# A scan kernel in rounds of six segments: the output projection and its addition one segment earlier, and tanh rows and two copies at other places on ScalarE

## The chip, the cores and the metric

The kernel runs on one core of one Trainium2 chip. The metric is device time in microseconds, the median of several executions. TensorE is called PE in the profile, VectorE DVE, ScalarE ACT, GpSimd POOL and SyncE SP.

## The reference

The input x is 8 sequences of 512 steps with 128 channels. The first layer is a selective state space block, the second a mixture of 16 experts. Both are added to x. What matters here is the first:

```python
x = layernorm(x)
xn = x * rsqrt(mean(x * x) + 1e-6) * norm_w
x_branch, gate = split(xn @ W_in.T)              # 256 and 256 channels
xc = silu(causal_conv(x_branch) + conv_b)
dt = soft_clamp(softplus(xc @ W_dt.T + b_dt), 0.001, 0.1, 0.5)
Bp, Cp = xc @ W_B.T, xc @ W_C.T                  # 16 states
dA = exp(soft_clamp(dt[..., None] * A, -8, 8, 0.5))   # soft_clamp is a tanh
def step(h, ...):                                # 512 steps, one after the other
    h = h * dA_t + dt_t * B_t * x_t              # h: 8 x 256 channels x 16 states
    nrm = sqrt(sum(h * h))                       # of each sequence
    h = where(t % 10 == 0, h * min(20 / nrm, 1), h)
    y = einsum('bdn,bn->bd', h, C_t) + D * x_t
x_out = y * silu(gate) @ W_out.T
return x + scale * x_out
```

Then x + x_out is normalised, routed by `Wg` to one expert each, and goes through `w1`, relu and `w2`.

## The kernel before

Every tenth step h is scaled by a factor of its own norm, so time is cut into 52 **segments** of 10 steps (the last has 2). Channels lie on the 128 partitions in two halves; with 16 states and 8 sequences there are 256 rows of state, each of 10 columns and one for the start value. Six segments make a **round** (`w`, 0 to 8; `s` is the segment's place in it, 0 to 5), and each round prepares the input of the next one (`v1`) and the one after that (`v2`), and finishes the output of the one before (`o = w - 1`).

One segment S runs like this. POOL forms B times u for segment S+1 in two products (`products`, L837), and multiplies the last states of segment S-1 by C (`c_last`, L851). ScalarE makes the decays in four pieces, `decay`, each an exp (L977) of what a row tanh (`row_tanh`, L1086) left in `z`. VectorE runs four scans (L1359), the first two of which find their decays ready, then gates y of S-1 (L1344), multiplies states by C (L1410), and reduces the norm (L1327). Before that ScalarE squares the last column in two pieces (L987), the second behind scan 3, and TensorE sums the squares over partitions (`norm_sum`, L1723). POOL takes the power -1/2 (`root`, L866), TensorE spreads the factor (`norm_spread`, L1729), and VectorE writes the new start values (`restart`, L1333), with which the next segment's scans begin. TensorE also sums the states of S-1 to y (`sum_y`, L1751 and L1763) ahead of the norm sum.

Every engine has one queue in the order in which the code is written, and waits on semaphores. There is no planner: the `if s == ...` branches in each engine's loop decide between which steps of the recurrence the work of the other rounds stands. That work is, for the parts that the change touches:

- `project_out(o)` (L1681): eight products of 128 columns of the gated y with `W_out`, on TensorE, into PSUM bank PA. It waits for the last gated y of round o and for the first dt tanh of `v1`, which reads that bank.
- `add_out(o)` (L1422): residual plus scaled projection, on VectorE, between the last C multiplications. Then `out_stats(o)`: mean and variance (L1257, L1262) between scan 0 and scan 1, and `out_pool(o)` on POOL between the two products: an add, a multiply, a power (L873) and a multiply (L875). `make_h2(o)` (L1059) on ScalarE uses them in s4.
- `ln_pool(v2, part)`: the same kind of small steps for the input's two norms; part 3 is L800 and L802.
- `evac_bc(v1)`: two copies (L1031, L1035) of B and C from PSUM, on ScalarE, between the fourth exp and the clamp of dt (L1046).
- Row tanhs: 32 rows a round. Half of them (`WHOLE`) are done once for all 60 steps, the others (`HALVES`) in two halves of 30.

TensorE's clock is kept up by products whose result nobody reads (`keep_clock`, L1746; `idle_products`, L1578) in s3, in segment 2 and in the last rounds.

Of the kernel before, what the change touches and what calls it, by code (L numbers as in the profile page):

```python
# [35 lines left out]
def mamba_moe(nc, x, norm_w, W_in, conv_w, conv_b, W_dt, b_dt, W_B, W_C, A_log, D_param, W_out,  # L36
# [8 lines left out]
    NWIN = (NSEG + SPW - 1) // SPW  # L45
# [27 lines left out]
    with ExitStack() as ctx:  # L73
# [217 lines left out]
        o = 0  # L291
        xs, o = take(z, o, E, CT, 2 * DM)
# [478 lines left out]
        def _(pool):  # L771
# [137 lines left out]
            for S in range(NSEG):  # L909
                w, s = place_of(S)  # L910
                v1, v2, o = w + 1, w + 2, w - 1
                if S > 0:
                    c_last(S - 1)
                if s == 5 and v1 < NWIN:
                    make_u(v1, 1)
                if v2 < NWIN:
                    if s == (0 if w > 0 else 1):
                        ln_pool(v2, 0)
                        ln_pool(v2, 1)
                    if s == (1 if w > 0 else 2):  # L920
                        ln_pool(v2, 2)
                    if s == 2:
                        ln_pool(v2, 3)
                if s == 4 and v1 < NWIN:
                    make_u(v1, 0)
                if S + 1 < NSEG:
                    products(S + 1, [0])
                    if s == 3 and v1 < NWIN:
                        split_c(v1)
                    if s == 3 and 0 <= o < NWIN - 2:  # L930
                        out_pool(o)
                    products(S + 1, [1])
                    root(S + 1)
# [6 lines left out]
        def _(act):  # L940
# [27 lines left out]
            def decay(G):  # L968

                S, g = G // NG, G % NG  # L970
                w, s = place_of(S)
                r0, r1 = GRAN[g]
                if s % HALF == 0:
                    act.wait_ge(tanh_done, max(tanh_at[w, k, s // HALF] for k in range(r0 // B, (r1 - 1) // B + 1)))
                at_least(act, gscan, G - 1)
                n = LAST_STEPS - 1 if S == LS else SEG
                act.activation(region(G)[:, 0:(r1 - r0) * SLOT].rearrange("p (r c) -> p r c", c=SLOT)[:, :, 1:1 + n],  # L977
                               zall[:, r0:r1, SEG * s:SEG * s + n], ACT.Exp, scale=16.0).then_inc(exp_done, 1)
# [117 lines left out]
            def first_half(v, k0, k1):  # L1096
                for k in HALVES[k0:k1]:
                    row_tanh(v, k, 0, HALF * SEG)

            def second_half(v, k0, k1):  # L1100
                for k in (list(range(NST)) if v == 0 else HALVES)[k0:k1]:
                    row_tanh(v, k, HALF * SEG, WIN)
# [5 lines left out]
            def opening_rows(k0, k1, t1):  # L1108
                for k in range(k0, k1):
                    row_tanh(0, k, 0, t1)  # L1110
# [28 lines left out]
            for S in range(NSEG):  # L1139
                w, s = place_of(S)  # L1140
                v1, v2, o = w + 1, w + 2, w - 1
                prep, ln, out_ = v1 < NWIN, v2 < NWIN, o >= 0

                if S == 0:
                    opening_rows(16, 27, WIN)
                decay(NG * S + 2)
                if S == 0:
                    opening_rows(27, 32, WIN)
                decay(NG * S + 3)

                if s == 0 and w > 0:
                    if prep:
                        silu_x(v1, 1)
                    second_half(w, 0, 2)
                elif s == 1 and prep:
                    half_tanh_dt(v1, 0)
                    half_tanh_dt(v1, 1)
                elif s == 2 and prep:
                    evac_bc(v1)
                    clamp_dt(v1)  # L1160
                elif s == 3:
                    if prep:
                        tanh_gate(v1, 0)
                        tanh_gate(v1, 1)
                    if w == NWIN - 1:
                        make_h2(o)
                    first_half(v1, 0, 1)
                elif s == 4 and out_:
                    make_h2(o)
                elif s == 5:  # L1170
                    whole(v1, 5, 7)

                if S + 1 < NSEG:
                    square_last(S, 0)

                if S == 0:
                    silu_x(1, 0)
                elif s == 0:
                    second_half(w, 2, 3)
                elif s == 1:  # L1180
                    second_half(w, 14, 15)
                elif s == 3:
                    first_half(v1, 1, 3)
                elif s == 4:
                    first_half(v1, 15, 16)
                elif s == 5:
                    whole(v1, 7, 8)

                if S + 1 < NSEG:
                    square_last(S, 1)  # L1190

                if S == 0:
                    silu_x(1, 1)
                if s == 5:
                    whole(v1, 8, 9)
                if s == 3 and ln:
                    evac_xT(v2)
                if s == (3 if w == NWIN - 1 else 4) and out_:
                    evac_h2T(o)

                if S + 1 < NSEG:
                    decay(NG * S + 4)
                    decay(NG * S + 5)

                if s == 0:
                    second_half(w, 0 if w == 0 else 3, 14)
                elif s == 1:
                    if prep:
                        log_dt(v1)
                    second_half(w, 15, 16)  # L1210
                elif s == 2:
                    if prep:
                        scale_dt(v1)
                    if ln:
                        norm_x(v2)
                        add_norm(v2)
                elif s == 3:
                    first_half(v1, 3, 15)
                elif s == 4:
                    if ln:  # L1220
                        silu_x(v2, 0)
                    whole(v1, 0, 5)
                elif s == 5:
                    whole(v1, 9, 16)

            evac_h2T(NWIN - 1)
            act_tail(act)
# [2 lines left out]
        def _(dve):  # L1230
# [270 lines left out]
            for S in range(NSEG):  # L1501
# [11 lines left out]
                    continue  # L1513

                scan(S, 0)
                if s == 3 and 0 <= o < NWIN - 2:
                    out_stats(o)
                scan(S, 1)
                if S == 0:
# [16 lines left out]
                n0 = 6  # L1536
                if S == 0:
                    make_xc(1, 0)
                elif s == 2 and out_ and w < NWIN - 1:
                    add_out(o)  # L1540
                elif s == 3 and prep:
                    make_gate(v1, 1)
                elif s == 4 and w + 3 < NWIN:
                    ln_in(w + 3)
                elif s == 5 and v2 < NWIN:
                    make_xc(v2, 0)
# [16 lines left out]
        def _(pe):  # L1563
# [235 lines left out]
            for S in range(NSEG):  # L1799
# [28 lines left out]
                if s == 0 and w > 0 and prep:  # L1828
                    project_dt(v1, 0, 0)
                    project_dt(v1, 1, 0)  # L1830
                if s == 2 and out_:
                    project_out(o, 0, TILES if w < NWIN - 1 else 2)
                if s == 3 and ln:
                    keep_clock(CBANK[1], S)
# [82 lines left out]
```

## Time and profile before

| | |
|---|---|
| median of 3 timed runs | 703.77 us (703.64 to 707.52) |
| profiled execution, its own time | 705.44 us |
| its span | 703.6 us |
| PE busy | 619.2 us (88%) |
| POOL busy | 580.6 us (83%) |
| DVE busy | 556.6 us (79%) |
| ACT busy | 518.4 us (74%) |
| mean granted clock of TensorE | 0.956 |

The span runs from the first instruction to the last. The recurrence runs from 35 us (the first L866) to about 573 us (the last); the experts follow. A share of busy time is a mean over stages, and TensorE's is made of pipelined products whose ends are modelled, so it doesn't say which engine sets the time. For that one has to see, segment by segment, who waits. The granted clock is given as a share of full speed: 1.00 is 2.4 GHz, 0.50 is 1.2 GHz.

### The profile page before, as it was taken

To read this page: it belongs to the slowest core of one execution; us is meant where nothing else is said; L and a number is where in the kernel's file an instruction comes from. 1 tells how busy PE (TensorE), PEld (TensorE's weight loads), DVE (VectorE), ACT (ScalarE), POOL (GpSimd) and SP (SyncE) were. 2 spreads that over 40 slices of the span, in tenths; PEclk is the share of its full clock that TensorE was granted. 3 is DMA by queue.
4 is the path that set the end of the run, shared out by engine and by line. 5 is a ranking of instruction groups with operands and counts; after the bars stand their busy time and mean duration, and the time that the engine had idled before them with its cause. 6 is when DMAs were issued, how large, how long until landed. Compare 5 with 4: busy or idle time off the path is not lost.

```text
span 703.6 us, 12853 instructions
## 1 busy us (share of the span) xinstructions
PE 619.2 (88%) x4108; PEld 479.8 (68%) x4108; DVE 556.6 (79%) x891; ACT 518.4 (74%) x1011; POOL 580.6 (83%) x411
## 2 busy tenths in 40 slices
PE   8589999999899999989999998989989894699774
PEld 6246666767677677767677677857767782589664
DVE  5567888999999999999999999989889985713221
ACT  3798978989989998998999899899978622112120
POOL 5088998999999999999999989999989971277775
PEclk9889989999999999999999999999999997599997
DMA  3241523226244423623441353316145304346541
GB/s 100 83 149 60 170 94 118 73 93 222 63 147 125 144 53 119 190 96 133 110 148 62 131 161 125 118 45 187 60 119 156 94 1 104 113 130 202 182 145 33
DMA packets 59978, 81.95 MB, mean 116 GB/s; under 512 B 14830, under 2 KB 40723, under 8 KB 59911
## 3 DMA queue, kind: packets, MB, share of 16 engines
q1 hardware_dynamic: 56400, 74.79, 34.1%
q0 software_dynamic: 2560, 6.08, 2.9%
q8 instruction: 33, 0.54, 0.3%
q10 hardware_dynamic: 950, 0.27, 0.2%
q14 instruction: 35, 0.28, 0.2%
HBM read 69.61 MB, written 11.72 MB: 116 GB/s over the span
## 4 chain that ended last, share of the span: by engine, by line
POOL 58%; issue 22%; PE 11%; DVE 4%; DMA 3%; POOLq 1%; ACTq 0%; SPq 0%; ACT 0%; DVEq 0%
POOL h L837 29%; POOL h L851 18%; POOL u L824 3%; PE ps L588 3%; PE ps L575 3%; POOL fac L866 1%; DMA z<-rows_d,gidx 1%; POOL lnp L798 1%; POOL rstd L873 1%; PE ps L1635 1%; PE ps L595 1%; POOL out_dram L398 1%; POOL cq L861 1%; PE ps L555 1%; POOL z L390 1%
## 5 line engine op out<-in xcount | busy, mean ns | idle before, releaser
L1359 DVE TENSOR_TENSOR_SCAN h<-ps,h 128x902 f32<-128x902 f32 x204 | 319.8, 1608 | 24.3 <-ACT ps L977 16.2
L837 POOL TENSOR_TENSOR h<-u,scr 128x1280 f32<-128x1280 f32 x104 | 283.6, 2744 | 2.4
L1751 PEld LDWEIGHTS ps<-h,ident 128*128 128x128 f32 x1632 | 225.2, 190 | 22.3 <-issue 17.8
L1751 PE MATMUL ps<-h,ident 128*128 128x160 f32 x1632 | 231.4, 300 | 1.1 <-issue 0.8
L1086 ACT ACTIVATE z<-dtb,asc 128x240 f32<-128x240 f32 (+3 forms) x432 | 201.6, 537 | 0.1
L977 ACT ACTIVATE ps<-z 128x820 f32<-128x820 f32 (+1 forms) x208 | 137.9, 687 | 32.4 <-DVE h L1359 28.7
L851 POOL TENSOR_TENSOR h<-h,scr 128x1280 f32<-128x1280 f32 (+1 forms) x52 | 138.0, 2655 | 0.7 <-DVE h L1375 0.7
L1410 DVE TENSOR_TENSOR h<-h,ps 128x640 f32<-128x640 f32 (+1 forms) x155 | 87.8, 577 | 0.5 <-issue 0.2
L1635 PE MATMUL ps<-xnT,wT 128*128 128x488 f32 x144 | 75.2, 636 | 0.0
L987 ACT ACTIVATE sqb<-h 128x208 f32<-128x208 f32 x102 | 44.9, 441 | 24.3 <-DVE h L1359 21.6
L390 POOL DMA_INDIRECT z<-rows_d,gidx x32 | 33.2, 1036 | 34.7 <-DVE gidx L496 25.3
L1723 PEld LDWEIGHTS ps<-sqb,sel 128*8 128x8 f32 x832 | 28.4, 90 | 47.0 <-ACT sqb L987 36.4
L1723 PE MATMUL ps<-sqb,sel 128*8 128x33 f32 x832 | 35.1, 195 | 28.6 <-ACT sqb L987 18.7
L866 POOL TENSOR_TENSOR fac<-s,neghalf_e 8x1 f32<-8x1 f32 x52 | 27.5, 530 | 34.2 <-DVE s L1327 33.4
L424 ACT COPY h<-ps 128x256 f32<-128x256 f32 x16 | 6.0, 373 | 60.0 <-PE ps L563 60.0
L1729 PEld LDWEIGHTS ps<-ident,fac 8*128 8x128 f32 x104 | 15.8, 189 | 39.7 <-POOL fac L866 36.8
L398 POOL DMA_INDIRECT out_dram<-z,sidx x32 | 32.0, 1000 | 12.6 <-issue 7.8
L1333 DVE SCALAR_TENSOR_TENSOR h<-ps,h 128x256 f32<-128x256 f32 x52 | 32.0, 615 | 11.6 <-PE ps L1729 11.1
L513 DVE TENSOR_SCALAR h<-ps 128x512 f32<-128x512 f32 x16 | 11.1, 692 | 34.4 <-PE ps L575 34.4
L1635 PEld LDWEIGHTS ps<-xnT,wT 128*128 128x128 f32 x144 | 27.1, 204 | 16.0 <-issue 14.1
L1654 PE MATMUL ps<-xc,wT 128*128 128x488 f32 x72 | 35.8, 621 | 0.4 <-DVE xc L1316 0.4
L824 POOL TENSOR_TENSOR u<-dtb,xc 128x488 f32<-128x488 f32 x18 | 22.2, 1234 | 16.0 <-DVE h L1489 16.0
(201 smaller groups left out, 812.8 us busy)
## 6 DMA issues: line engine op xcount, KB each, us to landing
scr<-b_d SPq DMA_DIRECT2D x52, 640.0 KB, 4.4
scr<-c_d SPq DMA_DIRECT2D x52, 320.0 KB, 4.2
z<-in_L_ffn_w_dram SPq DMA_DIRECT2D x32, 256.0 KB, 3.2
xx_d<-xx SPq DMA_DIRECT2D x8, 256.0 KB, 2.0
xxr<-xx_d SPq DMA_DIRECT2D x8, 256.0 KB, 2.6
rows_d<-h2b SPq DMA_DIRECT2D x16, 120.0 KB, 2.1
rows_d<-xxr SPq DMA_DIRECT2D x16, 120.0 KB, 2.2
out_dram<-xxr SPq DMA_DIRECT2D x16, 120.0 KB, 2.4
```

The lines of the kernel that those rows point to most:

```text
L390: pool.indirect_dma_start(xs[:, e, t, :], None, rows_d, bass.IndirectOffsetOnAxis(ap=gidx[:, i:i + 1], axis=0), bounds_check=TOK - 1, oob_ ...
L824: pool.tensor_tensor(u[:, v % 2, hf, :], dtb[:, v % 2, hf, :], xc[:, v % 3, hf, :], ALU.mult).then_inc(u_done, 1)
L837: pool.tensor_tensor(hr[:, hf * RH:(hf + 1) * RH, 1:SLOT].rearrange("p (n b) t -> p n b t", b=B), us.unsqueeze(1).to_broadcast([P, NST, B, ...
L851: pool.tensor_tensor(m, m, cc4[:, S % RING, :].rearrange("p (r t) -> p r t", t=SEG)[:, :, 0:n] .unsqueeze(1).to_broadcast([P, H, NP * B, n ...
L977: act.activation(region(G)[:, 0:(r1 - r0) * SLOT].rearrange("p (r c) -> p r c", c=SLOT)[:, :, 1:1 + n], zall[:, r0:r1, SEG * s:SEG * s + n ...
L987: act.activation(sq_r[:, r0 // B:r1 // B, :], rows(h, S % RING)[:, r0:r1, SEG].rearrange("p (r b) -> p r b", b=B), ACT.Square).then_inc(sq ...
L1086: act.activation(zrow[:, k, :, t0:t1], dtb[:, v % 2, hf, :].rearrange("p (b c) -> p b c", b=B)[:, :, 1 + t0:1 + t1], ACT.Tanh, scale=asc[: ...
L1359: dve.tensor_tensor_scan(hs, region(G)[:, 0:(r1 - r0) * SLOT], hs, 0.0, ALU.mult, ALU.add).then_inc(gscan, 1)
L1410: dve.tensor_tensor(m, m, ps[:, bk, c0:c0 + (n1 - n0) * BS].rearrange("p (r t) -> p r t", t=SEG)[:, :, 0:n] .unsqueeze(1).to_broadcast([P, ...
L1635: ins = pe.matmul(bankc((PA, PB)[hf]), wT[:, hf * TAPS + k, :], xnT[:, :, k:k + COLS], start=False, stop=(k == TAPS - 1))
L1723: ins = pe.matmul(ps[0:B, YB, NCOL:NCOL + SQC], sel[:, b, :], sq_b[:, b, :], start=(b == 0), stop=(b == B - 1))
L1751: pe.matmul(ps[:, YB, 0:H * BS], ident[:], hr[:, :, n * B:(n + 1) * B, 0:SEG], start=(n == 0), stop=False)
```

## The change

For rounds 1 to 7, `project_out` moves from s2 to s1, with `add_out` behind it, and the statistics (`out_stats`, `out_pool`) from s3 to s2 (rounds 1 to 7). The last two steps of `ln_pool` follow its third directly, in s1 for s2. On ScalarE the copies of B and C move ahead of the fourth exp of s2, two whole row tanhs come from s5 to ahead of the fourth exp of s0, and half rows move: out of s3's long run and of s0 before the squares, into s5 and s1. The same instructions are issued in all, on every engine.

```diff
@@ ln_pool(v2, 3) on POOL
                     if s == (1 if w > 0 else 2):
                         ln_pool(v2, 2)
-                    if s == 2:
                         ln_pool(v2, 3)
@@ POOL
-                    if s == 3 and 0 <= o < NWIN - 2:
+                    if s == 2 and 0 <= o < NWIN - 2:
                         out_pool(o)
@@ ScalarE, before the fourth exp
+                elif s == 0:
+                    whole(w, 14, 16)
+                elif s == 2 and prep:
+                    evac_bc(v1)
                 decay(NG * S + 3)
@@ ScalarE, behind it
                     if prep:
                         silu_x(v1, 1)
-                    second_half(w, 0, 2)
...
                 elif s == 2 and prep:
-                    evac_bc(v1)
                     clamp_dt(v1)
...
-                    first_half(v1, 0, 1)
@@ ScalarE, between the squares
-                    second_half(w, 2, 3)
+                    second_half(w, 0, 1)
                 elif s == 1:
-                    second_half(w, 14, 15)
+                    second_half(w, 14 if w == 0 else 12, 15 if w == 0 else 13)
                 elif s == 3:
-                    first_half(v1, 1, 3)
+                    first_half(v1, 0, 2)
                 elif s == 4:
-                    first_half(v1, 15, 16)
+                    first_half(v1, 12, 13)
@@ ScalarE, behind the next segment's first two exps
-                    second_half(w, 0 if w == 0 else 3, 14)
+                    second_half(w, 0 if w == 0 else 1, 14 if w == 0 else 12)
                 elif s == 1:
...
-                    second_half(w, 15, 16)
+                    second_half(w, 15 if w == 0 else 13, 16)
...
-                    first_half(v1, 3, 15)
+                    first_half(v1, 2, 12)
...
-                    whole(v1, 9, 16)
+                    whole(v1, 9, 14)
+                    first_half(v1, 13, 16)
@@ VectorE
-                if s == 3 and 0 <= o < NWIN - 2:
+                if s == 2 and 0 <= o < NWIN - 2:
                     out_stats(o)
...
-                elif s == 2 and out_ and w < NWIN - 1:
+                elif s == 1 and out_ and w < NWIN - 1:
                     add_out(o)
@@ TensorE
-                if s == 2 and out_:
+                if s == (1 if w < NWIN - 1 else 2) and out_:
                     project_out(o, 0, TILES if w < NWIN - 1 else 2)
```

TensorE, s1 and s2 of a middle round, before: in s1 the dt products (L1654) of s0, the sum of states, two spreads of C (L1738), the norm sum (L1723), and the products for B and C (L1664); then s2 with the projection (L1681) ahead of its norm sum and the gate product (L1649).

```order
L1654 MATMUL ps<-xc,wT 128x488 x2
L1751 MATMUL ps<-h,ident 128x160 x16
L1763 MATMUL ps<-xc,diag_d 128x80 x2
L1738 MATMUL ps<-c,ones_b 128x480
L1738 MATMUL ps<-c,ones_b 128x160
L1723 MATMUL ps<-sqb,sel 8x33 x8
...
L1751 MATMUL ps<-h,ident 128x160 x16
L1763 MATMUL ps<-xc,diag_d 128x80 x2
L1738 MATMUL ps<-c,ones_b 128x480
L1681 MATMUL ps<-wT,yg 128x128 x8
L1723 MATMUL ps<-sqb,sel 8x33 x8
```

The same place after, where every line number is one lower or higher (L1682 is the projection):

```order
L1655 MATMUL ps<-xc,wT 128x488 x2
L1752 MATMUL ps<-h,ident 128x160 x16
L1764 MATMUL ps<-xc,diag_d 128x80 x2
L1739 MATMUL ps<-c,ones_b 128x480
L1739 MATMUL ps<-c,ones_b 128x160
L1682 MATMUL ps<-wT,yg 128x128 x8
L1724 MATMUL ps<-sqb,sel 8x33 x8
...
L1752 MATMUL ps<-h,ident 128x160 x16
L1764 MATMUL ps<-xc,diag_d 128x80 x2
L1739 MATMUL ps<-c,ones_b 128x480
L1724 MATMUL ps<-sqb,sel 8x33 x8
```

The eight products went from between the sum of states and the norm sum of s2 to the same place in s1.

VectorE, from the end of s1 into s2, before: the reduction (L1327), C multiplications (L1410), restart (L1333) and scans (listed as L1359).

```order
L1327 TENSOR_REDUCE s<-ps 8x1
L1410 TENSOR_TENSOR h<-h,ps 128x2x16x10 x2
L1333 SCALAR_TENSOR_TENSOR h<-ps,h 128x256
L1359 SCALAR_TENSOR_TENSOR h<-ps,h 128x902
L1359 SCALAR_TENSOR_TENSOR h<-ps,h 128x506
L1359 SCALAR_TENSOR_TENSOR h<-ps,h 128x902
L1359 SCALAR_TENSOR_TENSOR h<-ps,h 128x506
```

And after, with the addition (L1423) and the statistics (L1258, L1263):

```order
L1328 TENSOR_REDUCE s<-ps 8x1
L1411 TENSOR_TENSOR h<-h,ps 128x2x16x10
L1423 SCALAR_TENSOR_TENSOR xxr<-ps,rs,xxr 128x512
L1411 TENSOR_TENSOR h<-h,ps 128x2x16x10
L1334 SCALAR_TENSOR_TENSOR h<-ps,h 128x256
L1360 SCALAR_TENSOR_TENSOR h<-ps,h 128x902
L1258 BN_STATS bst<-xxr 128x6 x4
L1261 MEMSET pad 128x1
L1263 BN_AGGR mv<-bst 128x2 x4
L1360 SCALAR_TENSOR_TENSOR h<-ps,h 128x506
L1360 SCALAR_TENSOR_TENSOR h<-ps,h 128x902
L1360 SCALAR_TENSOR_TENSOR h<-ps,h 128x506
```

The addition now stands ahead of the restart of s2, the statistics between its first two scans.

ScalarE, from the end of s5 into s0, before: whole row tanhs, the two exps (L977), the tanh of x (L1011), two half rows and the first squares (L987).

```order
L1086 ACTIVATE z<-dtb,asc 128x480 x7
L977 ACTIVATE ps<-z 128x82x10
L977 ACTIVATE ps<-z 128x46x10
L1011 ACTIVATE thx<-ps 128x488
L1086 ACTIVATE z<-dtb,asc 128x8x30 x2
L987 ACTIVATE sqb<-h 128x26x8
```

And after:

```order
L1085 ACTIVATE z<-dtb,asc 128x480 x5
L1085 ACTIVATE z<-dtb,asc 128x8x30 x3
L976 ACTIVATE ps<-z 128x82x10
L1085 ACTIVATE z<-dtb,asc 128x480 x2
L976 ACTIVATE ps<-z 128x46x10
L1010 ACTIVATE thx<-ps 128x488
L986 ACTIVATE sqb<-h 128x26x8
```

Two whole rows moved from before the two exps to between them, and the tanh of x stands behind them.

## Rows read from the trace of the kernel before

**Rows 1.** The page, part 4: the chain that ended last, by engine.

```profile
POOL 58%; issue 22%; PE 11%; DVE 4%; DMA 3%; POOLq 1%; ACTq 0%; SPq 0%; ACT 0%; DVEq 0%
```

**Rows 2.** Timeline, POOL, segments 25 to 30: start, length (us), operation, [idle before].

```profile
315.05 0.53 POOL L866 TENSOR_TENSOR fac<-s,neghalf_e 8x1 f32<-8x1 f32 x1
...
325.03 0.53 POOL L866 TENSOR_TENSOR fac<-s,neghalf_e 8x1 f32<-8x1 f32 x1 [0.80 <-DVE s L1327]
...
331.67 0.20 POOL L870 TENSOR_TENSOR ve<-mv,eps 128x4 f32<-128x4 f32 x1
...
333.22 2.74 POOL L837 TENSOR_TENSOR h<-u,scr 128x1280 f32<-128x1280 f32 x1
336.30 0.53 POOL L866 TENSOR_TENSOR fac<-s,neghalf_e 8x1 f32<-8x1 f32 x1 [0.34 <-DVE s L1327]
...
346.91 0.53 POOL L866 TENSOR_TENSOR fac<-s,neghalf_e 8x1 f32<-8x1 f32 x1 [0.83 <-DVE s L1327]
...
357.30 0.53 POOL L866 TENSOR_TENSOR fac<-s,neghalf_e 8x1 f32<-8x1 f32 x1 [0.48 <-DVE s L1327]
...
367.71 0.53 POOL L866 TENSOR_TENSOR fac<-s,neghalf_e 8x1 f32<-8x1 f32 x1
```

**Rows 3.** Timeline of PE (TensorE), segments 25 to 27, same columns.

```profile
314.09 0.66 PE L1723 MATMUL ps<-sqb,sel 128*8 128x33 f32 x16 [0.85 <-ACT sqb L987]
...
322.09 2.05 PE L1681 MATMUL ps<-wT,yg 128*128 128x128 f32 x16
324.07 0.66 PE L1723 MATMUL ps<-sqb,sel 128*8 128x33 f32 x16
...
335.35 0.66 PE L1723 MATMUL ps<-sqb,sel 128*8 128x33 f32 x16 [0.72 <-ACT sqb L987]
```

**Rows 4.** Timeline of DVE (VectorE), segments 25 to 30.

```profile
316.12 0.61 DVE L1333 SCALAR_TENSOR_TENSOR h<-ps,h 128x256 f32<-128x256 f32 x1 [0.36 <-PE ps L1729]
...
320.26 3.14 DVE L1359 TENSOR_TENSOR_SCAN h<-ps,h 128x902 f32<-128x902 f32 x2 [0.26 <-ACT ps L977]
...
326.33 0.60 DVE L1333 SCALAR_TENSOR_TENSOR h<-ps,h 128x256 f32<-128x256 f32 x1
...
329.01 0.85 DVE L1257 BATCH_NORM_STATS2 bst<-xxr 128x6 f32<-128x128 f32 x4
...
330.19 3.10 DVE L1359 TENSOR_TENSOR_SCAN h<-ps,h 128x506 f32<-128x506 f32 x2
...
342.44 3.14 DVE L1359 TENSOR_TENSOR_SCAN h<-ps,h 128x902 f32<-128x902 f32 x2 [0.88 <-ACT ps L977]
...
364.62 0.64 DVE L1316 SCALAR_TENSOR_TENSOR xc<-thx,ps 128x488 f32<-128x488 f32 x1
```

**Rows 5.** Timeline of ACT (ScalarE), segments 26 to 30.

```profile
322.81 0.92 ACT L987 ACTIVATE sqb<-h 128x208 f32<-128x208 f32 x2
...
336.93 4.74 ACT L1086 ACTIVATE z<-dtb,asc 128x240 f32<-128x240 f32 x12
...
363.06 0.55 ACT L1011 ACTIVATE thx<-ps 128x488 f32<-128x488 f32 x1
```

**Rows 6.** Windows (busy by engine, PEclk, DMA share, GB/s); then PE, POOL timeline.

```profile
91.80:95.20 3.40, 1.97 (x27) 1.46 (x25) 3.27 (x5) 2.11 (x5) 2.71 (x2) 1.00 0.00 0
95.20:102.00 6.80, 6.80 (x13) 3.38 (x13) 6.15 (x16) 4.97 (x9) 6.56 (x4) 0.50 0.43 149
...
399.00:402.40 3.40, 3.40 (x6) 1.33 (x5) 2.36 (x5) 3.40 (x9) 3.40 (x3) 0.50 0.08 18
...
94.40 0.66 PE L1723 MATMUL ps<-sqb,sel 128*8 128x33 f32 x16 [1.43 <-ACT sqb L987]
...
107.99 0.53 POOL L866 TENSOR_TENSOR fac<-s,neghalf_e 8x1 f32<-8x1 f32 x1 [2.73 <-DVE s L1327]
...
410.01 0.53 POOL L866 TENSOR_TENSOR fac<-s,neghalf_e 8x1 f32<-8x1 f32 x1 [1.50 <-DVE s L1327]
...
525.48 0.53 POOL L866 TENSOR_TENSOR fac<-s,neghalf_e 8x1 f32<-8x1 f32 x1 [1.89 <-DVE s L1327]
```

## The prediction

> **What bounds the kernel now.** I read three views. The chain that ended last is POOL for 58% of the span and "issue" for 22% [rows 1]: the two state products and the C product of each of 52 segments. But the chain alone misleads, so I went to the timeline of one round (segments 24 to 29, the fifth round). POOL's power L866 ends each segment, and its row tells who was late. I call its start the root, R, and the segments of a round s0 to s5. Where the row has no idle time, POOL was just in time or late itself; where it says "DVE s L1327", the recurrence was late: restart L1333, four scans L1359, squares on ACT, norm sum L1723 on PE, reduction L1327. From [rows 2], the root waits 0.80 us in s2, 0.34 in s3, 0.83 in s4, 0.48 in s5, and nothing in s1 and s0. So the work of POOL and the recurrence lie within a few tenths of each other everywhere, and anything put on the recurrence in any segment, or on POOL in s0 or s1, costs its full length. The segments last (root to root) 9.98 us in s2, 11.27 in s3, 10.61 in s4, 10.39 in s5, 10.41 in s0. s3 is the longest, and loses most to what the change takes out of it. Rounds 1 to 7 of 0 to 8 have the moved projection.
>
> **Projection to s1 (seven rounds).** Its eight products lie from 322.09 to the norm sum at 324.07, so they cost TensorE 1.98 us [rows 3]. In s2 they were nearly free: the squares end at 322.81 + 0.92 = 323.73 [rows 5], so the norm sum came only about 0.3 late. In s1 TensorE starts its sum of states later, since the dt products precede it, and had just 0.85 us idle before the norm sum at 314.09 [rows 3]. The projection needs only the first dt tanh and the last gated y of the round before, both there by then, and it is issued ahead of the norm sum on an engine that runs products in order. The norm sum, and behind it reduction, root and restart, come 1.98 - 0.85 = 1.13 us later; I take **+1.1** for s1. The two small POOL steps that come to s1 too (each like the 0.20 us add of 331.67 [rows 2], about 0.5 with issue) would by themselves have lengthened s1; behind 1.1 they are free.
>
> **Addition to s1, statistics to s2.** The addition stands between the last C multiplications and the restart. In s2 the restart began 326.33 - 325.03 = 1.30 after the root, in s1 316.12 - 315.05 = 1.07 [rows 2, 4]. So the addition brings s2 at most 0.23. What it gives back in s3 is nothing that I count, because TensorE's two gate products around the root set the restart there too. The statistics, between scan 0 and scan 1, take 330.19 - 329.01 = 1.18 us of VectorE [rows 4]. In s2 they come on top, but two waits go: 0.3 for the projection, and the wait of scan 2 for ScalarE's exp (0.26 idle in the row of 320.26, 0.37 with the pieces around it). Result on the recurrence: 1.18 + 0.23 - 0.3 - 0.37 = **+0.75**. POOL's statistics steps take 333.22 - 331.67 = 1.55 [rows 2]; against the 0.80 that POOL waits in s2, and the 0.5 that left for s1, they are +0.25 and covered. If the waits did not go, s2 would grow by 1.4; if the exp were late by the two more row tanhs, no more than that, as they run while VectorE does restart and scan 0, and TensorE's lateness in s1 has given ScalarE 1.1 us.
>
> **s3.** It loses 1.18 of statistics and, on POOL, 1.55. Without them POOL needs 11.27 - 0.34 - 1.55 = 9.4 and isn't the bound. The recurrence gets the 1.18, less a few hundredths in which ScalarE (its eight normalisations now stand directly before the exp of scan 2) may be late: **-1.15**.
>
> **ScalarE rows.** Twelve half rows ran before the exp of scan 2 in s4: 4.74 us, 0.395 each, and VectorE waited 0.88 for that exp [rows 4, 5]. Two leave: 2 x 0.395 = 0.79 < 0.88, and POOL would allow 0.83: **-0.79** in s4. They go to s5 (five whole and three half rows for seven whole: 3.0 + 1.2 = 4.2 us, the same) and s1. In s0 two whole rows (1.2 us) now stand before the second exp and the tanh of x. That tanh ran at 363.06 for 0.55 [rows 5]; it would end about 364.8, and the multiplication L1316 that waits for it began at 364.62 [rows 4], so it begins about 364.9: **+0.28**, with no slack to hide it in (the root of 367.71 did not wait, and POOL had only just finished). The copies of B and C move ahead of the second exp of s2, for which VectorE isn't ready until scan 1 ends. They and the clamp took 322.81 - 320.26 = 2.55 us at most [rows 4, 5]; in the new order the clamp ends before scan 2 does, so they cost nothing. If they did delay the squares, as much as 0.5 would show in s2.
>
> **Sum with the clock unchanged.** A round: 0.28 + 1.1 + 0.75 - 1.15 - 0.79 = +0.19. Rounds 1 to 6 give +1.1. Round 7 has no gain in s4 (POOL bounds it there): +1.0. Round 0 has only the row tanhs: -0.8. Together **+1.3 us**.
>
> **The clock.** In s2 TensorE now finishes its sums at about R + 7.0 (where the projection began, 322.09 - 315.05) and has nothing until the norm sum at R + 10.73 - 0.96 = R + 9.8: an idle stretch of **2.7 us**, in seven rounds. The windows view shows what shorter ones did. TensorE idled 1.43 us before the norm sum of 94.40, and the granted clock was 0.50 (1.2 GHz) from 95.20 to 102.00; after waits like the 0.72 of 335.35 it mostly stayed at 1.00, but one such round was at 0.50 from 399.00 to 402.40 [rows 3, 6]. What it cost is in the root's waits: 2.73 for 0.48 at 107.99, so 2.25 us; 1.50 for 0.83 at 410.01, so 0.7; and 1.89 for 0.34 at 525.48, so 1.55 [rows 2, 6]. A new fall of 3.4 us at half clock delays TensorE's work by up to 1.7 us. Of that s3 hides little, since without the statistics the sum of states, the clock keeper and the turn of x fill the time to the norm sum (its 0.72 shrinks to about 0.4): 1.3 each, between 0.7 (the row at 410.01) and 1.7. I take six falls in seven rounds: 6 x 1.3 = +7.8. The old three mostly go: s4 of round 0 is 0.79 shorter, with an idle stretch of 0.6 for 1.43 (-2.25); round 7 waited in s3 for a gate that now comes 1.15 earlier (-1.55); the third I count by half (-0.35). Net +3.7. The Trainium skill (TensorE: Matmul & The Clock Gate, Why this matters for your kernels) puts a fall down to a window in which TensorE is idle. Taken literally that would spare s2, where TensorE works on both sides of the gap; the row of 91.80 to 95.20, busy for 1.97 us of 3.40 ahead of a fall [rows 6], speaks against that reading. By the page the result would be the rival without falls.
>
> **Result.** +1.3 + 3.7 = +5. On the profiled execution, 705.44 us (its span 703.6 and 1.8 around it), that is 710.4. That execution lies 1.7 above the median of the three timed runs, 703.77; on the median it is 708.8, so **709 us**, with a range of its own of 705 to 713. A measurement of this kernel can tell about 1% (7 us) from no change.
>
> **Rivals.** (1) No falls, as the idle stretch is short of what the clock tolerates: 703.8 + 1.3 - 4.15 = **701**. For it: most 0.7 us waits cost nothing. Against: 1.43 did. (2) Slower: long falls. If a fall begins before the norm sum of s2 it still has idle time behind it, and then lasts 6.8 us like the one from 95.20; it halves the norm sum and both gate products around the root. Price up to 3.4 us less 0.4 a round; with four long and three short ones 4 x 3.0 + 3 x 1.3 = 15.9, so 703.8 + 1.3 + 15.9 - 4.15 = **717**. It decides from the point where the onset comes ahead of the norm sum. (3) Faster: the projection in s1 is hidden after all (TensorE gets through the sum of states earlier), 7 x 1.1 = 7.7 less than (1): **693**. For it only that the first tanh of dt is done early; against it TensorE's unbroken row of work before 0.85. (4) The change doesn't do what it says: a wait in s1 (for the residual's load or PSUM bank) keeps the addition late. The order shows the edits on all engines and the load is issued a segment earlier, so this stays small; with it every figure in s2 grows by a few tenths: 712.
>
> **Chances.** Forecast 0.47, (1) 0.22, (2) 0.18, (3) 0.08, (4) 0.05. Faster by over 1% (below 696.7) is (3) and a sliver of (1): 0.09. Slower by over 1% (above 710.8) is (2), a third of the forecast, and most of (4): 0.39. Within 1%: 0.52. The range for 8 in 10 leaves out (3) and the far end of (2): 699 to 718.
>
> **What would show it.** Root to root in a middle round: s1 about 10.8 (from 9.74), s2 10.7, s3 10.1 without a fall and 11.4 with one, s4 9.8, s0 10.7. The norm sum of s2 with some 2.7 us of idle TensorE before it, that of s1 directly behind the projection with none. A clock row with several slices below 9 between the start and the end of the recurrence. VectorE's 0.88 for the exp in s4 gone. I am wrong if the norm sum of s1 still waits for the squares, if s3 doesn't shrink by about 1.1, or if the clock holds through s2.

## The result, and the profile after

The changed kernel takes 713.5 us (median of 4 runs, 710.26 to 716.11); the kernel before, on the same chip, 704.16 (703.64 to 707.52, 4 runs). The ratio is 1.0129 [1.0076, 1.0182]: slower by 1.3%, about 9 us, just outside the 1% that the prediction took as what a measurement can tell. Forecast were 709, with 0.52 on "within 1%" and 0.39 on slower. One execution of a later kernel, e7_keep_silu, took 904.6 us at a mean granted clock of 0.644, and is left out of every range and ratio below.

| | before | after |
|---|---|---|
| profiled execution, its own time | 705.44 us | 710.26 us |
| its span | 703.6 | 708.5 |
| mean granted clock of TensorE | 0.956 | 0.951 |
| start of the last root | 572.82 | 577.80 |

The profiled execution of the changed kernel is the fastest of its four, while that of the kernel before lies 1.7 us above its median. So the two traces differ by 5 us and the medians by 9; the gap is taken up below.

The page after, its clock slices (part 2) and the chain that ended last (part 4), the latter beside [rows 1]:

```profile
PEclk9889999899999999999999899999999997599997
...
POOL 60%; issue 21%; PE 10%; DMA 4%; DVE 4%; POOLq 1%; ACTq 0%; SPq 0%; ACT 0%; DVEq 0%
```

The chain has nearly the same shares as before and says nothing of the change. The roots do. POOL's timeline, L866 from the end of s0 of round 2 to the end of s0 of round 3; start, length, operation, [idle before]:

```profile
179.42 0.53 POOL L866 TENSOR_TENSOR fac<-s,neghalf_e 8x1 f32<-8x1 f32 x1 [0.53 <-DVE s L1328]
...
190.22 0.53 POOL L866 TENSOR_TENSOR fac<-s,neghalf_e 8x1 f32<-8x1 f32 x1 [0.53 <-DVE s L1328]
...
200.93 0.53 POOL L866 TENSOR_TENSOR fac<-s,neghalf_e 8x1 f32<-8x1 f32 x1 [0.53 <-DVE s L1328]
...
211.00 0.53 POOL L866 TENSOR_TENSOR fac<-s,neghalf_e 8x1 f32<-8x1 f32 x1 [0.68 <-DVE s L1328]
...
220.84 0.53 POOL L866 TENSOR_TENSOR fac<-s,neghalf_e 8x1 f32<-8x1 f32 x1
...
231.23 0.53 POOL L866 TENSOR_TENSOR fac<-s,neghalf_e 8x1 f32<-8x1 f32 x1 [0.47 <-DVE s L1328]
...
242.01 0.53 POOL L866 TENSOR_TENSOR fac<-s,neghalf_e 8x1 f32<-8x1 f32 x1 [0.51 <-DVE s L1328]
```

Differences of these starts are the segments of an undisturbed round, against those that [rows 2] and the prediction give:

| segment | before | predicted | after | change, predicted | change, measured |
|---|---|---|---|---|---|
| s1 | 9.74 | 10.8 | 10.80 | +1.1 | +1.06 |
| s2 | 9.98 | 10.7 | 10.71 | +0.75 | +0.73 |
| s3 | 11.27 | 10.1 | 10.07 | -1.15 | -1.20 |
| s4 | 10.61 | 9.8 | 9.84 | -0.79 | -0.77 |
| s5 | 10.39 | 10.4 | 10.39 | 0 | 0 |
| s0 | 10.41 | 10.7 | 10.78 | +0.28 | +0.37 |

Without the clock a round grows by 0.19, as priced. The mechanisms are those that the prediction named, too. TensorE after, norm sums of s1, s2 and s3 of round 2, beside [rows 3]:

```profile
187.28 2.05 PE L1682 MATMUL ps<-wT,yg 128*128 128x128 f32 x16
...
189.26 0.66 PE L1724 MATMUL ps<-sqb,sel 128*8 128x33 f32 x16
...
199.97 0.66 PE L1724 MATMUL ps<-sqb,sel 128*8 128x33 f32 x16 [2.45 <-ACT sqb L986]
...
210.04 0.66 PE L1724 MATMUL ps<-sqb,sel 128*8 128x33 f32 x16 [0.33 <-ACT sqb L986]
```

In s1 the projection now stands directly ahead of the norm sum, and the 0.85 us of idle time is gone. In s2 the stretch without work is 2.45 us (2.7 was forecast). VectorE, from the reduction of s1 to the statistics of s2, beside [rows 4]:

```profile
189.96 0.18 DVE L1328 TENSOR_REDUCE s<-ps 8x1 f32<-8x33 f32 x1 [1.19 <-PE ps L1724]
...
190.47 0.73 DVE L1423 SCALAR_TENSOR_TENSOR xxr<-ps,rs,xxr 128x512 f32<-128x512 f32 x1
...
191.52 0.60 DVE L1334 SCALAR_TENSOR_TENSOR h<-ps,h 128x256 f32<-128x256 f32 x1
...
194.20 0.85 DVE L1258 BATCH_NORM_STATS2 bst<-xxr 128x6 f32<-128x128 f32 x4
```

The restart begins 191.52 - 190.22 = 1.30 after the root, as forecast, and the statistics stand between scan 0 and scan 1. In s0 the tanh of x is late, on VectorE:

```profile
238.89 0.66 DVE L1317 SCALAR_TENSOR_TENSOR xc<-thx,ps 128x488 f32<-128x488 f32 x1 [0.26 <-ACT thx L1010]
```

What is not as priced is the clock. A fall is a stretch in which the granted clock is 0.50; in the recurrence of all traces here, behind the first 43 us, it lasts 3.4 us (short) or 6.8 us (long). Round 1 has a long one. The windows view around it (us; busy time of PE, PEld, DVE, ACT, POOL; clock; DMA share; GB/s), and in the last two lines a short one of round 3:

```profile
130.60:134.00 3.40, 1.68 (x13) 1.31 (x11) 3.40 (x3) 2.64 (x4) 3.32 (x6) 1.00 0.31 83
134.00:140.80 6.80, 6.07 (x26) 3.42 (x27) 4.42 (x8) 5.53 (x12) 5.88 (x4) 0.50 0.36 118
140.80:144.20 3.40, 3.40 (x27) 3.40 (x25) 3.40 (x3) 2.46 (x4) 3.24 (x4) 0.99 0.79 269
260.40:263.70 3.30, 1.13 (x18) 0.92 (x19) 3.17 (x6) 2.55 (x6) 2.77 (x2) 1.00 0.74 244
263.80:267.10 3.30, 3.30 (x6) 1.33 (x5) 1.91 (x4) 3.30 (x8) 3.30 (x3) 0.50 0.16 53
```

And what the long one does to TensorE around the root, and then to the roots of s2, s3 and s4:

```profile
134.73 1.05 PE L1724 MATMUL ps<-sqb,sel 128*8 128x33 f32 x16 [2.45 <-ACT sqb L986]
...
135.95 2.00 PE L1650 MATMUL ps<-xnT,wT 128*128 128x488 f32 x2
137.88 0.59 PE L1730 MATMUL ps<-ident,fac 8*128 8x8 f32 x2
```

```profile
136.07 0.53 POOL L866 TENSOR_TENSOR fac<-s,neghalf_e 8x1 f32<-8x1 f32 x1 [0.92 <-DVE s L1328]
...
148.13 0.53 POOL L866 TENSOR_TENSOR fac<-s,neghalf_e 8x1 f32<-8x1 f32 x1 [2.68 <-DVE s L1328]
...
158.25 0.53 POOL L866 TENSOR_TENSOR fac<-s,neghalf_e 8x1 f32<-8x1 f32 x1 [0.34 <-DVE s L1328]
```

At 1.2 GHz the norm sum takes 1.05 us for 0.66, and the gate products hold the spread of the factor back to 137.88. s2 is 11.09 long for 10.71, s3 148.13 - 136.07 = 12.06 for 10.07, s4 10.12 for 9.84: 0.38 + 1.99 + 0.28 = **2.65 us for a long fall**. Rounds 1 and 5 have one. Rounds 3 and 4 have a short fall that begins behind the norm sum (s3 11.26 and 11.30, s4 10.12: 1.5 each), and round 7 a short one that costs 1.15. Rounds 2 and 6 have none, though TensorE idles the same 2.45 us in them. The falls of this trace add up to 9.4 us in five rounds, against 7.8 in six. One more thing differs between the two traces, and has nothing to do with the moved work: the kernel before has a short fall at 54 to 58 us, in segment 1 of the opening (root to root 13.05 us), and the changed kernel has none there (11.37).

### The profile page after: what moved, and what is told of

Its sections match the earlier page's. It is cut to its first block, busy times and chain, and to the rows that moved or that the text cites. A ratio compares the mean times of both kernels' runs of the same rounds, so it can differ in the third digit from the quotient of the medians.

```text
span 708.5 us, 12846 instructions
## 1 busy us (share of the span) xinstructions
PE 623.9 (88%) x4108; PEld 483.1 (68%) x4108; DVE 556.5 (79%) x891; ACT 521.1 (74%) x1011; POOL 580.6 (82%) x411
## 4 chain that ended last, share of the span: by engine, by line
POOL 60%; issue 21%; PE 10%; DMA 4%; DVE 4%; POOLq 1%; ACTq 0%; SPq 0%; ACT 0%; DVEq 0%
POOL h L837 31%; POOL h L851 18%; POOL u L824 3%; PE ps L588 3%; PE ps L575 3%; DMA z<-rows_d,gidx 2%; POOL fac L866 1%; POOL lnp L798 1%; POOL rstd L873 1%; PE ps L1636 1%; POOL z L390 1%; PE ps L555 1%; POOL cq L861 1%; POOL out_dram L398 1%; DMA b0b<-b_d 1%
## 5 line engine op out<-in xcount | busy, mean ns | idle before, releaser
L1752 PEld LDWEIGHTS ps<-h,ident 128*128 128x128 f32 x1632 | 227.5, 192 | 25.3 <-issue 19.6
L1636 PE MATMUL ps<-xnT,wT 128*128 128x488 f32 x144 | 72.2, 613 | 0.0
L866 POOL TENSOR_TENSOR fac<-s,neghalf_e 8x1 f32<-8x1 f32 x52 | 27.6, 531 | 39.6 <-DVE s L1328 39.4
```

The source lines that it names most:

```text
L1636: ins = pe.matmul(bankc((PA, PB)[hf]), wT[:, hf * TAPS + k, :], xnT[:, :, k:k + COLS], start=False, stop=(k == TAPS - 1))
L1752: pe.matmul(ps[:, YB, 0:H * BS], ident[:], hr[:, :, n * B:(n + 1) * B, 0:SEG], start=(n == 0), stop=False)
```

## Experiments

The first four kernels ran on one chip, the last four on another. On the first chip the kernel before took 713.58 us (25 runs, 709.61 to 718.2) instead of 704. Segments without a fall were as long there as elsewhere; from the last root to the end of the span it took 141 to 143 us instead of some 131, and the totals of one kernel lay up to 9 us apart. There the roots of the profile decide, and the totals tell little. Neither the kernel before nor the changed one has a profile from that chip, so roots are compared across chips; on the second chip (703.81 us, 12 runs, 701.87 to 705.45) both can be used.

| run | what it is | median, us (range) | ratio to before, same chip | last root |
|---|---|---|---|---|
| e1_keep | changed, s2 kept busy | 714.05 (710.22 to 717.89) | 0.9997 [0.9966, 1.0028] | 570.18 |
| e2_act_only | ScalarE's part alone | 713.26 (709.85 to 716.61) | 0.9983 [0.9955, 1.0012] | 567.76 |
| e3_out_only | the rest alone | 733.29 (731.84 to 736.41) | 1.0273 [1.0224, 1.0322] | 588.12 |
| e4_proj_end | projection at the end of s1 | 720.08 (715.86 to 724.9) | 1.0086 [1.0051, 1.0122] | 578.6 |
| e0_before | kernel before, one look | 705.89 | | 573.94 |
| e5_changed | the changed kernel | 711.96 (710.36 to 713.33) | 1.0117 [1.0085, 1.0149] | 579.01 |
| e6_two_rows | before, two half rows moved | 697.0 (695.84 to 700.7) | 0.9916 [0.9889, 0.9942] | 563.51 |
| e7_keep_silu | e1_keep, tanh of x first | 699.41 (697.52 to 702.1) | 0.9948 [0.9925, 0.9972] | 565.84 |

**e1_keep: is it the idle stretch of s2?** The changed kernel, with TensorE given products that nobody reads in that stretch.

```diff
+                if s == 2 and 0 < w < NWIN - 1:
+                    keep_clock(CBANK[1], S)
+                    keep_clock(CBANK[1], S)
```

> The changed kernel with two clock-keeping products of 512 columns (1.1 us each by the row of L1746) in s2 of rounds 1 to 7, between the spread of C and the norm sum, where TensorE is idle for 2.7 us. Theory (the loss beside the sum of the segments is TensorE's clock falling in that idle stretch): no falls in rounds 1 to 7, s1 10.8, s2 10.7, s3 10.1, s4 9.8 in every round, and about 701 us, 12 below the changed kernel and 3 below the one before. Rival (the clock is a symptom and the time is lost to the waits that were moved): about 713 as the changed kernel. If the products run into the norm sum, s2 grows by some tenths.

The idle stretch before the norm sum shrinks from 2.45 to 0.54 us. TensorE, s2 of round 2:

```profile
195.37 1.98 PE L1747 MATMUL ps<-wT,ones_w 128*128 128x512 f32 x4
197.89 0.66 PE L1724 MATMUL ps<-sqb,sel 128*8 128x33 f32 x16 [0.54 <-ACT sqb L986]
```

In rounds 1 to 6 no segment shows a fall any more: s1 10.80, s2 10.70, s3 10.07, s4 9.84 in each. Round 7 has none in s2 to s4 either, but one in s5 (11.10 us long; the clock is at 0.50 from about 534 to 537), which the expectation did not have. The clock slices show it:

```profile
PEclk9889999999999999999999999999999995799896
```

Its last root comes at 570.18, 7.6 us ahead of the changed kernel's 577.80, although its opening (segments 0 and 1) was 1.1 us longer. Adding that 1.1 and the 1.25 of the fall in s5 of round 7, less 0.55 for a first root that came earlier, gives 9.4, which is what the falls of the changed kernel's trace add up to. The filler delays nothing: s2 is as long as in an undisturbed round of the changed kernel. The total missed what was expected of it. Its level, 714 for 701, is the chip's, but the ratio missed too: 0.9997 where 3 us less than the kernel before were expected. The totals of that chip cannot tell the two apart well, and the same edit is timed again in e7_keep_silu.

**e2_act_only: ScalarE's part alone.** The kernel before, with ScalarE's hunks of the diff and nothing else.

```diff
@@ ScalarE: every hunk of the change; TensorE, VectorE and POOL as before
+                elif s == 0:
+                    whole(w, 14, 16)
+                elif s == 2 and prep:
+                    evac_bc(v1)
                 decay(NG * S + 3)
...
```

> The kernel before with only the changes on ScalarE (row tanhs, copies of B and C). Theory: s4 9.84 (-0.77), s0 10.77 (+0.36), the other segments as before, the fall of round 0 gone (-2.6 in s5): 704.2 - 0.8 - 2.6 - 6 x 0.41 + 0.4 = about 699 us. Rival (the rows in s1 and the copies ahead of the fourth exp cost the recurrence in s2): s2 10.3 to 10.8, and 701 to 704.

s4 is 9.84 and s0 10.77, as in the changed kernel, and no segment of rounds 1 to 7 shows a fall. But s2 is 10.46, not 9.98: there the rival was right. ScalarE, ahead of the exp of scan 2 in s2, then VectorE and POOL:

```profile
191.24 0.48 ACT L1086 ACTIVATE z<-dtb,asc 128x240 f32<-128x240 f32 x1
191.63 0.84 ACT L977 ACTIVATE ps<-z 128x820 f32<-128x820 f32 x1
```

```profile
192.49 3.14 DVE L1361 TENSOR_TENSOR_SCAN h<-ps,h 128x902 f32<-128x902 f32 x2 [1.03 <-ACT ps L977]
```

```profile
186.50 0.53 POOL L866 TENSOR_TENSOR fac<-s,neghalf_e 8x1 f32<-8x1 f32 x1
...
196.97 0.53 POOL L866 TENSOR_TENSOR fac<-s,neghalf_e 8x1 f32<-8x1 f32 x1 [1.28 <-DVE s L1329]
```

Before, scan 2 of s2 waited 0.26 for that exp and began 320.26 - 315.05 = 5.21 after the root [rows 2, 4]; here it waits 1.03 and begins 192.49 - 186.50 = 5.99 after it, since two more half rows stand ahead of the exp. In the changed kernel nobody notices: the root of s1 comes a microsecond later there, and the statistics keep VectorE busy in the meantime. The prediction had used that cover for its s2; the expectation for this run forgot that it goes when the ScalarE part stands alone. A term that is free only behind another term of the same change has to be priced again when the other is taken out.

**e3_out_only: the rest alone.** The changed kernel with ScalarE as before.

```diff
@@ TensorE, VectorE and POOL as in the change; ScalarE as before
-                if s == 2 and out_:
+                if s == (1 if w < NWIN - 1 else 2) and out_:
                     project_out(o, 0, TILES if w < NWIN - 1 else 2)
...
```

> The kernel before with only the changes on TensorE, VectorE and POOL (projection, addition, statistics, last norm steps), ScalarE as before. Theory: s1 10.8, s2 10.7 to 10.9, s3 10.1 without a fall and 11.3 to 12.1 with one, s4 stays 10.6, s0 10.4. 704.2 + 7 x 0.7 + falls of about 7 less 1.5 in round 7 = about 714 us. Rival (the row changes cause the falls or the late s1): about 704.

Undisturbed, s1 is 10.80, s2 10.78, s3 10.07, s4 10.61 and s0 10.41: the terms are additive where no cover is shared. The total is 19.7 us above the kernel before, where 10 were expected, and most of it is the clock. POOL, the ends of s2 to s5 of round 5:

```profile
395.45 0.53 POOL L866 TENSOR_TENSOR fac<-s,neghalf_e 8x1 f32<-8x1 f32 x1 [0.62 <-DVE s L1326]
...
408.34 0.53 POOL L866 TENSOR_TENSOR fac<-s,neghalf_e 8x1 f32<-8x1 f32 x1 [3.51 <-DVE s L1326]
...
419.23 0.53 POOL L866 TENSOR_TENSOR fac<-s,neghalf_e 8x1 f32<-8x1 f32 x1 [1.12 <-DVE s L1326]
...
432.88 0.53 POOL L866 TENSOR_TENSOR fac<-s,neghalf_e 8x1 f32<-8x1 f32 x1 [3.76 <-DVE s L1326]
```

s3 is 12.89 for 10.07, and s5 432.88 - 419.23 = 13.65 for 10.39: one segment loses 3.3 us, more than any of the changed kernel. Both are long falls, from 395 and from 419 us. That the second comes from the idle stretch of s4, which is long again with VectorE's wait for the exp, is my reading; no run varies that stretch alone. Read segment by segment, the falls of rounds 1 to 7 add up to 14.6 us in this kernel, against 9.4 in the changed one and 1.25 in e1_keep. The changed kernel differs from this one by ScalarE's part alone, so in these executions that part took some of the falls away.

**e4_proj_end: projection in the idle stretch of s1's end instead.** The changed kernel with the eight products behind the last product of s1, after the spread, and the addition in s2 between scan 0 and the statistics.

```diff
@@ TensorE
-                if s == (1 if w < NWIN - 1 else 2) and out_:
-                    project_out(o, 0, TILES if w < NWIN - 1 else 2)
+                if s == 2 and out_ and w == NWIN - 1:
+                    project_out(o, 0, 2)
...
+                if s == 1 and out_ and w < NWIN - 1:
+                    project_out(o, 0, TILES)
@@ VectorE: add_out(o) from s1 to s2, ahead of out_stats(o)
```

> The changed kernel with the projection behind the last product of s1 (after the norm spread) in place of ahead of the norm sum, and the addition in s2 between scan 0 and the statistics. Theory: s1 back to 9.8, s2 11.2 (the addition now lies between scans, +0.5), TensorE's sum of states in s2 starts 2 us later and fills the idle stretch down to 0.7 us, so no falls; s3 10.1, s4 9.8: 704.2 - 7 x 0.38 - 4.2 = about 697 us. Rival (TensorE is the bound in s2 once the projection precedes the sum of states): s2 over 11.5 and no gain over the kernel before.

This failed. TensorE and POOL, round 2:

```profile
192.03 1.95 PE L1681 MATMUL ps<-wT,yg 128*128 128x128 f32 x16
193.82 4.51 PE L1751 MATMUL ps<-h,ident 128*128 128x160 f32 x32
...
200.59 0.66 PE L1723 MATMUL ps<-sqb,sel 128*8 128x33 f32 x16 [1.55 <-ACT sqb L986]
```

```profile
190.21 0.53 POOL L866 TENSOR_TENSOR fac<-s,neghalf_e 8x1 f32<-8x1 f32 x1
...
201.55 0.53 POOL L866 TENSOR_TENSOR fac<-s,neghalf_e 8x1 f32<-8x1 f32 x1 [1.07 <-DVE s L1328]
```

TensorE is busy at the right place, but 1.55 us of idle time stay ahead of the norm sum (0.7 was expected), and s3 is 11.26 to 12.62 long in five rounds of seven: the falls did not go. s2 is 201.55 - 190.21 = 11.34 with the addition in it. And in rounds 2 to 6 s1 shrinks only to 10.22, since POOL ends it without idle time: the two small steps of `ln_pool`, 0.48 us, of which the prediction said "behind 1.1 they are free", are not free once the 1.1 is gone.

**e0_before and e5_changed: both kernels again**, on the chip of the last four.

> The kernel before, once more, for a second profile of it on the chip of this call. Theory: every segment as in the first profile (s1 9.74, s2 9.98, s3 11.27, s4 10.61, s5 10.39, s0 10.41) but for those in which TensorE's clock falls, which change place or go; the part behind the recurrence is about 10 us longer on a chip like that of the first call. Rival: the segments themselves differ by chip.

> The changed kernel, once more, beside the kernel before on one chip. Theory: slower by 0.5 to 1.3% with falls in four to seven of the rounds 1 to 7, all of them begun between the end of the sums of s2 and the middle of s3; s1 10.80, s2 10.71 or 11.1, s3 10.07, 11.3 or 12.1. Rival (the first result came from the chip or from chance): within 0.3% of the kernel before.

The kernel before repeats the segments of its first profile, from segment 1 on, within 0.04 us where no fall is, and has its falls in the same segments, each to 0.1 us; it shows one more, in s5 of round 7. From its last root to the end it takes 130 us, so this chip lacks the 11 us that the first of the two added there. The changed kernel is 8.15 us slower, 1.0117 [1.0085, 1.0149], with falls in rounds 1, 3, 4, 5 and 7 again, the long ones in 1 and 5 again. So in rounds 1 to 7 the places of the changed kernel's falls are the same in two executions. That is not so everywhere: this execution also has the fall at 53 to 57 us, in segment 1 (12.81 us), which the first trace of the same kernel lacks. The executions at a lower mean clock (down to 0.942) have no trace here.

**e6_two_rows: the one part that gains, without the rest.** The kernel before with two of the twelve half rows that stand ahead of the exp of scan 2 in s4 moved to ahead of the fourth exp of s3. There ScalarE waits for VectorE anyway.

```diff
+                elif s == 3:
+                    first_half(v1, 13, 15)
                 decay(NG * S + 3)
...
-                    first_half(v1, 3, 15)
+                    first_half(v1, 3, 13)
```

> The kernel before with one edit: two of the twelve half-row tanhs of s3's long run stand ahead of the fourth exp of s3, where ScalarE was idle for 1.42 us. Theory: the wait of 0.88 us in s4 falls to 0.1 at no price, s4 9.84 in rounds 0 to 6, all else as before: 7 x 0.77 = 5.4 us less, and 2.6 less if the fall of round 0 went with it, so 0.8 to 1.1% faster than the kernel before. Rival (the rows delay the gate's tanhs and the fourth exp in s3): s3 above 11.3 and no gain.

It is faster than both kernels. ScalarE in s3 and s4 of round 2, and the roots of s2, s3 and s4:

```profile
200.15 0.87 ACT L1086 ACTIVATE z<-dtb,asc 128x240 f32<-128x240 f32 x2
201.63 0.56 ACT L977 ACTIVATE ps<-z 128x460 f32<-128x460 f32 x1 [0.61 <-DVE h L1361]
...
207.09 3.97 ACT L1086 ACTIVATE z<-dtb,asc 128x240 f32<-128x240 f32 x10
```

```profile
195.19 0.53 POOL L866 TENSOR_TENSOR fac<-s,neghalf_e 8x1 f32<-8x1 f32 x1 [0.78 <-DVE s L1329]
...
206.47 0.53 POOL L866 TENSOR_TENSOR fac<-s,neghalf_e 8x1 f32<-8x1 f32 x1 [0.36 <-DVE s L1329]
...
216.31 0.53 POOL L866 TENSOR_TENSOR fac<-s,neghalf_e 8x1 f32<-8x1 f32 x1
```

After the two rows ScalarE still waits 0.61 us for VectorE in s3, so they cost s3 nothing (11.28 as before); s4 is 216.31 - 206.47 = 9.84 for 10.61. That is 0.77 in each of rounds 0 to 6, 5.4 in all of the 6.8 between the medians. The other 1.4 I put down to the clock, without a run that shows it alone: the falls of round 0 and of 399 [rows 6] are gone, and that of round 7, 3.4 us long before, is a long one from 513.4 (s3 11.73, s4 11.08), which costs 1.8 for 1.5.

**e7_keep_silu: what is left of the changed kernel without falls.** e1_keep, with the tanh of x ahead of the two whole rows in s0.

```diff
+                    if prep:
+                        silu_x(v1, 1)
                     whole(w, 14, 16)
                 decay(NG * S + 3)
...
-                if s == 0 and w > 0:
-                    if prep:
-                        silu_x(v1, 1)
-                elif s == 1 and prep:
+                if s == 1 and prep:
```

> The changed kernel with the two clock-keeping products in s2 and, in s0, the tanh of x ahead of the two whole rows. Theory: s0 back to 10.41, so 7 x 0.36 = 2.5 us less than with the products alone, no falls in rounds 1 to 6; last power at about 567 to 568 us in the profile, and 0.3 to 0.5% faster than the kernel before. Rival (the whole rows before the fourth exp delay scan 3 then): s0 10.7.

s0 is back at 238.32 - 227.93 = 10.39. POOL's roots, ends of s5 of round 2 and of s0 and s1 of round 3:

```profile
227.93 0.53 POOL L866 TENSOR_TENSOR fac<-s,neghalf_e 8x1 f32<-8x1 f32 x1 [0.48 <-DVE s L1327]
...
238.32 0.53 POOL L866 TENSOR_TENSOR fac<-s,neghalf_e 8x1 f32<-8x1 f32 x1
...
249.13 0.53 POOL L866 TENSOR_TENSOR fac<-s,neghalf_e 8x1 f32<-8x1 f32 x1 [0.54 <-DVE s L1327]
```

No round shows a fall. The kernel takes 699.41 us, 12.55 less than e5_changed on the same chip. Of that 7 x 0.37 = 2.6 is s0, and the rest, **10.0 us, is what falls cost the changed kernel** (to some 3 us, by the intervals of the two ratios). The trace of e5_changed agrees: the segments in which falls lengthen rounds 1 to 7 add up to 9.6.

## Why the prediction was right in direction and too small

**The sum with the clock unchanged was right**, and so was its working. The projection in s1 cost 1.06 for 1.1, since TensorE had no slack but its 0.85. Statistics less the two waits gave 0.73 for 0.75, s3 -1.20 for -1.15, the row tanhs -0.77 for -0.79. Only s0 was off by more, 0.37 for 0.28, because the tanh of x ends a tenth later than forecast (7.6 us after the root of s5, for 7.5); with the small gains elsewhere the round is still +0.19. Rounds 1 to 6 give 1.1, round 7 +1.0 and round 0 -0.8: +1.3, as priced.

**The step that failed is the size of the term "The clock", net +3.7.** The changed kernel is 8.15 us slower on the second chip (6.0 to 10.5 by the interval of its ratio). Less 1.3 that leaves 6.9 for the clock (4.7 to 9.2), and 9.3 - 1.3 = 8.0 on the chip of the first result: both above 3.7. How it splits is read from e7_keep_silu. New falls cost 10.0, where 7.8 stood. And e7_keep_silu is the kernel before plus the round's sum without s0: -0.18 in rounds 1 to 6, +0.6 in round 7, -0.8 in round 0, together -1.3. So the kernel before would take 699.4 + 1.3 = 700.7 without falls, and its old falls cost 703.8 - 700.7 = 3.1 (0.7 to 4.0 by the interval of e7_keep_silu's ratio), where 4.15 were given back.

Three steps were off, the first two in that term, the third in how it was put on the median:

- "1.3 each": short falls cost 1.15 to 1.5, long ones 2.65, and two of five were long. This is the mechanism of rival (2), with fewer of them than it took (four) and at 2.65 instead of 3.0. The 0.28 that s4 still loses after a fall was in no step.
- "The old three mostly go", for 4.15: they do go, in both traces. But their price was read from one execution which, with 705.44 us, lay 1.7 above its median. In that trace the one of round 0 costs 1.9: it lengthens s5 by 2.6, and the next two segments give back 0.7 (s0 of round 1 is 10.21, and 10.75 in e6_two_rows, which lacks the fall). With 0.7 and 1.5 for the other two that is 4.1, so 4.15 was right for the trace. Over the twelve executions on the second chip the old falls are worth 3.1, with 4.15 at the edge of the interval.
- "On the profiled execution 710.4": that was met (710.26), but by an execution below the median of its own four. The step "on the median it is 708.8" took the old trace's offset for one that holds for both kernels. It has the other sign in the new one. And that 710.4 was met is luck: falls of 9.4 less 4.1, and 1.3, make 6.6 between the two traces, not 5.0; almost all of the rest is the opening, whose first root and segments 0 and 1 together came 1.5 us earlier in the new trace, where the fall of segment 1 is missing.

**Rival (1)**, no falls, is refuted for the kernel as changed: five rounds of seven have one, in both traces of it. Its time was not far off for the kernel in which they are taken away: it said 701, and e7_keep_silu, which also spares s0 its 2.6, has 699.4. The stretch ahead of the fall at 134.00 had TensorE busy for 1.68 of 3.40 us, that ahead of 263.80 for 1.13 of 3.30, so work on both sides of the gap did not spare s2. The Trainium skill (TensorE: Matmul & The Clock Gate, Why this matters for your kernels) puts a fall down to a window in which TensorE is idle. Taken literally, as in rival (1), that does not agree with this case's traces: in the two stretches just named TensorE worked for 1.68 and 1.13 us. **Rival (3)**, the projection hidden in s1, is refuted by an s1 of 10.80 us and the missing idle time ahead of its norm sum. **Rival (4)**, a late addition, is refuted too: the restart of s2 came 1.30 us after the root, as forecast.

**What stays open.** The same program position, with 2.45 us idle, gives a long fall in rounds 1 and 5, a short one in 3, 4 and 7, and none in 2 and 6. In the long ones of this kernel the clock drops before the norm sum, in the short ones behind it. That is no rule for the length, though: the long falls at 95.20 in the kernel before [rows 6] and at 395 in e3_out_only begin as the norm sum ends or just behind it. What decides where in the round the drop can begin was not varied by any run. So nothing in these runs would have let one compute the number and the kind of falls from the trace of before; they could only be bounded.

## What to carry to other kernels

Where two engines run within tenths of each other, the timeline of one round, read at the one instruction that closes each segment, prices a move of work to within 0.1 us a segment; a share of busy time doesn't. A move that takes work from TensorE needs a second price, that of the idle stretch which it leaves: here 2.45 us of idle TensorE cost more than all the rest of the change, and two products that nobody reads took the cost away. Take the useful part alone (e6_two_rows: two half rows into a place where ScalarE waits anyway) before spending cover elsewhere, and price clock falls over several executions, since one profile can lie on either side of its own median.

## What the runs showed of the hardware that was not expected

The clock did not answer to the length of the idle stretch alone: the same 2.45 us gave 0, 3.4 and 6.8 us at half clock, in the same rounds in two executions. A long fall costs 2.65 us in the changed kernel, and 3.3 in a single segment where it began at the root of s4 (s5 of round 5 in e3_out_only). Mean granted clock and time go together from execution to execution of the changed kernel: 710.26 us at 0.951, 712.18 at 0.949, 714.82 at 0.944, 716.11 at 0.942. And two chips differed in the part behind the recurrence: 141 to 143 us for 130 to 131, while the segments without a fall that their kernels share were the same to a few hundredths (s3 10.07 in e1_keep and e7_keep_silu).
